# Opening of a fused adaLN/FFN kernel: longer and earlier dummy products, attention spread on GpSimd, side columns last, four low pieces of B11

## What is computed

```python
# stage 1: a mixed 1x1 convolution, per batch entry b (128 of them), x is (128, 64, 1024)
h = gelu(cond @ W0 + b0)
h = gelu(h @ W1 + b1)
att = softmax(h @ W2 + b2)                       # (128, 8)
agg_w = einsum('bk,koi->boi', att, weight)       # a 64x64 matrix for each b
agg_b = att @ bias_k
y = einsum('boi,bih->boh', agg_w, x) + agg_b[:, :, None]
# stage 2: a linear layer with 8 LoRA experts, the best 2 weighted
base = einsum('bsd,od->bso', y, base_W)          # 1024 x 1024
logits = einsum('bsd,ed->bse', y, router_W)      # 8 experts
mid = einsum('bsd,edr->bser', y, lora_A) * w_dense[..., None]
out = x + base + 2 * einsum('bser,erd->bsd', mid, lora_B)
```

## Time and profile before

| what | us |
|---|---|
| median of 3 runs | 967.26 |
| lowest and highest | 966.91, 967.41 |
| the profiled execution, whole | 968.04 |
| its span (first to last instruction) | 966.3 |
| TensorE busy in the span | 954.1 |
| VectorE busy | 739.2 |
| GpSimd busy | 294.5 |
| ScalarE busy | 236.8 |

### The profile page before, as it was taken

How to read it: one execution, slowest core, us unless ns; L and a number is a source line. 1 busy time by engine, 2 the same in 40 slices (tenths; PEclk the granted TensorE clock), 3 DMA queues, 4 the chain that set the end, 5 groups by cost and what they waited for, 6 DMA issues and landing times.

```text
span 966.3 us, 17804 instructions
## 1 busy us (share of the span) xinstructions
PE 954.1 (99%) x5765; PEld 880.7 (91%) x5765; DVE 739.2 (76%) x1641; ACT 236.8 (25%) x541; POOL 294.5 (30%) x228
## 2 busy tenths in 40 slices
PE   8999899999999999999999999999999999999997
PEld 6998799999999999999999999999999999999996
DVE  5858878777778777778777778777788777787774
ACT  5435122222122222222222222222222222222210
POOL 3002331233331333321333321333322333322331
PEclk9999999999999999999999999999999999999999
DMA  8766143332343332343333343323342323432311
GB/s 341 190 199 179 51 136 115 111 117 89 114 136 111 112 106 100 114 136 110 113 101 105 114 135 107 115 95 106 119 135 98 122 89 104 131 128 96 131 47 44
DMA packets 46693, 116.04 MB, mean 120 GB/s; under 512 B 20432, under 2 KB 20560, under 8 KB 45520
## 3 DMA queue, kind: packets, MB, share of 16 engines
q1 hardware_dynamic: 45824, 111.54, 34.6%
q0 software_dynamic: 576, 4.19, 2.2%
q10 hardware_dynamic: 272, 0.03, 0.0%
HBM read 77.97 MB, written 33.59 MB: 115 GB/s over the span
## 4 chain that ended last, share of the span: by engine, by line
PE 95%; DVE 3%; issue 1%; ACT 0%; POOL 0%; DVEq 0%; POOLq 0%; ACTq 0%
PE pc L499 17%; PE pb L510 13%; PE pa L510 12%; PE y_ps L471 11%; PE pb L513 9%; PE pa L513 9%; PE pd L499 8%; PE pc L554 4%; PE pd L554 4%; PE pc L536 1%; PE pa L524 1%; PE pd L536 1%; PE pb L524 1%; PE pd L544 1%; DVE w_lo L928 1%
## 5 line engine op out<-in xcount | busy, mean ns | idle before, releaser
L471 PE MATMUL y_ps<-mix_w,x_sb 128*128 128x128 f32 x1024 | 194.9, 276 | 0.1
L394 POOL TENSOR_TENSOR out_sb<-out_sb,u 128x512 f32<-128x512 f32 x90 | 127.8, 1449 | 202.2 <-DVE u L1109 202.2
L471 PEld LDWEIGHTS y_ps<-mix_w,x_sb 128*128 128x128 f32 x1024 | 168.6, 191 | 12.8 <-DVE ya L1014 0.5
L364 POOL TENSOR_TENSOR ya<-ya 128x512 f32<-128x512 f32 x30 | 40.4, 1345 | 384.6 <-DVE ya L1014 384.6
L1014 DVE TENSOR_TENSOR ya<-y_ps,bias_sb 128x512 f32<-128x512 f32 x128 | 87.7, 685 | 39.2 <-PE y_ps L471 35.7
L499 PE MATMUL pc<-w_hi,s_hi 128*128 128x512 f32 x240 | 99.1, 413 | 0.0
L510 PE MATMUL pa<-w_hi,a_hi 128*128 128x376 f32 x240 | 94.6, 394 | 0.7 <-ACT p L825 0.7
L499 PE MATMUL pc<-w_hi,s_lo 128*128 128x512 f32 x240 | 94.4, 393 | 0.0
L499 PE MATMUL pc<-w_lo,s_hi 128*128 128x512 f32 x240 | 93.8, 391 | 0.0
L810 ACT ACTIVATE exps<-logits,neg_max 128x8 f32<-128x8 f32 x64 | 19.3, 301 | 271.3 <-DVE neg_max L1031 271.3
L817 ACT ACTIVATE mid_hi<-pd 128x128 fp32r<-128x128 f32 x62 | 17.2, 278 | 276.1 <-PE pd L544 276.1
(11 more groups left out here) (214 smaller groups left out, 2554.7 us busy)
## 6 DMA issues: line engine op xcount, KB each, us to landing
x_sb<-in_x SPq DMA_DIRECT2D x64, 512.0 KB, 3.9
out_sb<-in_x SPq DMA_DIRECT2D x64, 512.0 KB, 4.3
out<-out_sb SPq DMA_DIRECT2D x64, 512.0 KB, 2.7
w_raw<-in_base_t SPq DMA_DIRECT2D x5, 1024.0 KB, 12.3
w_raw<-neg POOLq DMA_DIRECT2D x4, 1024.0 KB, 11.4
bias_sb<-bias_rows SPq DMA_DIRECT2D x62, 64.0 KB, 4.9
w_raw<-in_side SPq DMA_DIRECT2D x1, 544.0 KB, 8.7
lb_raw<-in_lora_b SPq DMA_DIRECT2D x1, 512.0 KB, 15.0
```

The costliest lines, as they stand in the source:

```text
L364: nc.gpsimd.tensor_tensor(y_block(0, 1), y_block(0, 1), y_block(0, 0), ALU.subtract).then_inc(s3_set, 1)
L394: nc.gpsimd.tensor_tensor(o, o, u2[:, :], ALU.add).then_inc(done, 1)
L471: mm = nc.tensor.matmul(y_ps[q % 2][:, j * P:(j + 1) * P], x_sb[m][:, c * P:(c + 1) * P], mix_w[m][:, :], start=True, stop=True)
```

## The change

Five things, all in the opening:

1. **Dummy products.** TensorE's queue begins with three products of a constant zero tile (128 columns, float32), ahead of the wait for `hot`. `keep_warm` takes the column counts: behind the second layer (512, 256) in place of one of 512, behind the third four of 512 in place of three, a new one of 512 behind the transposed attention, (512, 256) in place of one behind the bias product, and the last two, which stood between the bias rows (L456) and the mixing, are gone.
2. **`att_spread` on GpSimd**, ahead of the split of B11, and no longer on VectorE (where it stood ahead of the first `add_bias`).
3. **Low part of B11 in four pieces** of 512 columns in place of two of 1024, each with its own count of `w_lo_set[B11]`.
4. **The first product of pair 0** does its twelve heads first, then waits for `side_lo_set`, and does its twelve tails.
5. **Bias rows.** Their DMA to DRAM goes from ScalarE's queue to SP's, behind the 12 loads; ScalarE sets both mixing blocks ahead of the copy of the bias.

```diff
@@ sync
+            sp.wait_ge(bias_ready, 1)
+            sp.dma_start(bias_dram.rearrange("s (b c) -> b s c", b=B),
+                         bias_rows[:, :].rearrange("b (s c) -> b s c", s=2)).then_inc(bias_out, 16)
             sp.wait_ge(bias_out, 16)
@@ gpsimd
+            pool.wait_ge(pick_set, 5)
+            pool.wait_ge(att_step, 4)
+            nc.gpsimd.tensor_tensor(att_spread[:, :].rearrange("j (t k) -> j t k", k=K),
+                                    own_tile[:, :].unsqueeze(2).broadcast_to([P, NT, K]),
+                                    att_n[:, :].unsqueeze(1).broadcast_to([P, NT, K]), ALU.mult).then_inc(spread_set, 1)
...
-            for n in range(WP):
-                pool.wait_ge(w_hi_set[B11], n + 1)
-                nc.gpsimd.tensor_tensor(w_lo[w_piece(B11, n)], w_raw[w_piece(T2, n)],
-                                        w_hi[w_piece(B11, n)].bitcast(f32), ALU.subtract).then_inc(w_lo_set[B11], 1)
...
+            for n in range(HALF):
+                if n % (HALF // WP) == 0:
+                    pool.wait_ge(w_hi_set[B11], n // (HALF // WP) + 1)
+                nc.gpsimd.tensor_tensor(w_lo[quarter(B11, n)], w_raw[quarter(T2, n)],
+                                        w_hi[quarter(B11, n)].bitcast(f32), ALU.subtract).then_inc(w_lo_set[B11], 1)
@@ tensor
+            def keep_warm(*columns):
+
+                for n in columns:
+                    nc.tensor.matmul(pb[:, 0:n], hot[:, 0:P], hot[:, 0:n], start=True, stop=True)
+
+            zeros = nc.const_aps.tensor(0.0, (P, P))
+            for _ in range(3):
+                nc.tensor.matmul(pb[:, 0:P], zeros, zeros, start=True, stop=True)
             pe.wait_ge(hot_set, 1)
...
-            keep_warm(1)
+            keep_warm(512, 256)
             pe.wait_ge(mlp_act, 2)
             nc.tensor.matmul(mlp_ps[1][:, 0:K], h2[:, :], w2_sb, start=True, stop=True).then_inc(mlp_mm, 1)
-            keep_warm(3)
+            keep_warm(512, 512, 512, 512)
...
             nc.tensor.transpose(mlp_ps[0][0:K, 0:B], att_n[:, :], ident[:, :]).then_inc(att_tr, 1)
+            keep_warm(512)
...
             nc.tensor.matmul(bias_ps, att_t[:, :], bk_sb[:, :], start=True, stop=True).then_inc(bias_mm, 1)
-            keep_warm(1)
+            keep_warm(512, 256)
             pe.wait_ge(bias_ready, 1)
...
             mm.then_inc(bias_bc_mm, 1)
-            keep_warm(2)
@@ plain_pair
                 if first(p):
+                    for j in range(HALF):
+                        pe.wait_ge(w_lo_set[B11], j + 1)
+                        for y, w, start, stop in plain_splits(*a11, j, True):
+                            plain_head(y, w, start, stop, B11, pa, j)
                     pe.wait_ge(side_lo_set, 1)
+                    for j in range(HALF):
+                        for y, w, start, stop in plain_splits(*a11, j, True):
+                            plain_tail(y, w, start, stop, B11, pa, j, 0)
@@ scalar
-            act.wait_ge(bias_ready, 1)
-            act.dma_start(bias_dram.rearrange("s (b c) -> b s c", b=B),
-                          bias_rows[:, :].rearrange("b (s c) -> b s c", s=2)).then_inc(bias_out, 16)
-            place_mix(0, 0)
+            for m in range(2):
+                place_mix(0, m)
             act.wait_ge(bias_bc_mm, 1)
...
-            place_mix(0, 1)
```

## The result

| | median, us | lowest to highest | executions |
|---|---|---|---|
| before, beside it | 967.39 | 966.67 to 968.49 | 20 |
| changed | 968.9 | 965.17 to 973.38 | 20 |

The ratio is 1.0019, with a 95% interval from 1.001 to 1.0028: the changed kernel is slower by about 0.2%, 1.5 us by the medians and 1.8 us by the ratio. The forecast was 965.6, and 963.5 to 967.0 the range. Half of the changed kernel's executions took 969.47 us or more, which no execution of before in that series did. The one that was profiled took 968.18, span 966.4; before's took 968.04.

The account below looks back on a forecast made before the run. TensorE was taken to bound the kernel, busy 954.1 of 966.3 us. Earlier mixing (-0.79) and no wait for the side columns (-0.90) gave -1.69 us, so 965.6 us, range 963.5 to 967.0.

Parts of the forecast that it names:

- Dummies ahead of the mixing: Opening on TensorE: two dummies gone, -1.00, 256 columns more earlier, +0.21; mixing starts at 12.82, 0.79 us earlier.
- Other dummies: Opening on TensorE: they fill pauses, taken as 0, up to +0.3 us if two tight places stick out.
- Side columns last: First product of pair 0: starts without waiting for side_lo, saving 0.90 us of a wait of 0.91.
- Attention on GpSimd: Ahead of B11's split: spread taken as 1.5 us, bounds 1.30 and 2.6, hidden; no gain by itself.
- The rival in which GpSimd's last piece stands in VectorE's way: Low part of A11 takes 1.3 us longer: 966.6; chance 0.06, shared with dummies that stick out.
- Bias rows on SP's queue: Pair 1's x tile 1 lands at 34.4, asked for at 35.0: hidden by 0.6 us, where it had 3.5.
- the sum: Whole execution: -0.79 and -0.90 make -1.69 us, median 967.26 to 965.6; chance 0.42.
- its upper bound, 10.5: Pair 1's x tile 1 takes 10.5 us, landing at 35.9; as a rival 966.5, chance 0.12.
- the slower rival: Pair 1's loads sink into the accumulating DMA: tile 1 lands at 39.3, 969.9 us; chance 0.08.
- the early rise: Denser dummies lift TensorE's clock before the mixing, 1.67 us more, gain cut by tile 1 to 2.3: 965.0; chance 0.14.
- The later fall of the clock: After TensorE's pause near 106 us: 1.7 us of work lost; a rival has it go away, 963.9, chance 0.18.

Follow-up runs that it names:

- e7: e1 with the two dummies of 512 columns ahead of the mixing put back; 964.84 us, ratio 0.9965.
- e5: e1 with the early dummies as before, the two ahead of the mixing still left out; 964.26 us, ratio 0.9969.
- e2: The kernel before with only the DMA of the bias rows moved to SP's queue behind the weight loads; 968.08 us, ratio 1.0005.
- e12: The kernel before with only heads first and tails last in the first product of pair 0; 966.0 us, ratio 0.9985.
- e6: e1 with heads and tails of the first product alternating again, waiting for side_lo, and the old dummies; 965.85 us, ratio 0.998.
- e1: The changed kernel with the DMA of the bias rows issued by ScalarE again; 964.06 us, ratio 0.9964.
- e11: e1 with the attention spread on VectorE again and B11's low part in two pieces; 963.13 us, ratio 0.9964.
- e13: The changed kernel as it is, first of four more executions looked at for the long times; 971.73 us.
- e16: The changed kernel as it is, fourth of four more executions looked at for the long times; 967.89 us.
- e3: The changed kernel with GpSimd's first accumulating DMA, and so both, held until x tile 1 of pair 1 has landed; 964.41 us, ratio 0.9964.
- e10: e1 with pair 1's x tiles issued before the wait for the bias rows and the first accumulating DMA behind x tile 1; 964.01 us, ratio 0.9965.
- e14: The changed kernel as it is, second of four more executions looked at for the long times; 970.39 us.
- e15: The changed kernel as it is, third of four more executions looked at for the long times; 970.51 us.
- e9: The changed kernel as it is, measured again for the spread; 967.83 us, ratio 1.0011, profiled execution 966.16 us.
- e17: The changed kernel with only GpSimd's second accumulating DMA held until x tile 1 of pair 1 is in; 968.66 us, ratio 1.0015.

## Why the prediction was wrong

**Dummies ahead of the mixing, -0.79: right.** Mixing at 12.88 in place of 12.82. In the time of an execution it can't be told from nothing (e7).

**Other dummies, 0: right** as far as the medians tell (e5). With them `pick_half` starts at 8.24 in place of 8.19, which is the 0.05 us of that tight place. Their effect on the clock stays open: with the new dummies it rose before 9 us in 8 of 15 traces, with the old ones in none of four (before, e2, e5, e12), which is too few to tell.

**Side columns last, -0.90: the place was right, the size perhaps too small.** In the profiled execution it gave what was said, since TensorE's own mixing was next. The runs give 1.3 to 1.5 us (e12) and 1.1 to 1.8 (e6 against e5 and e1), but e12's interval holds 0.90, and those of e5 and e6 overlap. What the term lacked is seen in e6's profile: it was read from an execution in which the clock rose at about 17 us. Where it rises early VectorE is the later of the two by more, the wait is 2.05 us, and 1.5 us of slow work follow.

**Attention on GpSimd, 1.5 us, hidden: right that it is hidden**, and 1.07 us is below the lower bound of 1.30. The rival in which GpSimd's last piece stands in VectorE's way didn't come in the first profile (VectorE's low part of A11 takes 0.69 us at 18.03). It did where the clock rose early: in e6 GpSimd's last piece ends at 16.3, and VectorE's row is

```profile
15.00 1.81 DVE L1049 TENSOR_TENSOR a_lo<-ya,a_hi 128x512 fp32r<-128x512 f32 x1 [0.69 <-ACT a_hi L836]
```

In e1 it takes 1.03 us. In e11, where GpSimd is done at 15.8, it takes 0.69.

**Bias rows on SP's queue, "hidden by 0.6 us": this step failed.** It had four numbers. The write was to land at 24.4; it did at 25.0 (e13: 24.7, e16: 24.4). The Trainium skill, "DMA: Bandwidth & Descriptors", section "Queues, rings and completion order", says that each DMA engine takes the descriptors of a ring in order, and the trace agrees: the 32 KB took 14.2 us behind the loads. Tile 1 was to be issued at 25.4 to 25.7; it was at 25.92. It was to need 8.7 us; it needed 10.9. And it was asked for at 35.2 in place of 35.0. Against the sum's 25.7 the issue is 0.2 us late, and the transfer 2.2 us long: tile 1 landed at 36.8 in place of 34.4, and a cover of 0.6 us became a wait of 1.63. The 8.7 us came from a transfer of before whose issue had stood in a full queue for 1.80 us; its upper bound, 10.5, was of the same transfer with that stand. The bound was taken for a worst case, but the tile here was issued 0.75 us after the accumulating DMA, and by e3 that DMA is worth 3.3 us of it. The sentence against the slower rival, "with the queue still full of weights, 10.5 us were enough", took a transfer whose issue began 1.8 us ahead of the accumulation's for one that is issued behind it.

**The sum was too small for the rest of the change.** Without the moved DMA the gain is 3.3 us by the medians and 3.5 by the ratio (e1), not 1.69; e11 and e10 say the same. Two of the rivals are in e1's profile together, the early rise and no fall behind the pause near 106 us: 3.77 us of lead at the pause, 5.2 at the end. How often each comes in executions without a trace isn't shown.

**The slower rival was the right mechanism**, at 0.08. It placed the break-even at 36.70, and mixing in the short executions starts at 36.27 to 36.85. It foresaw a landing at 39.3 and 969.9 us; the three long executions have 37.6 to 39.0 us and 970.4 to 971.7. The rest is what no case had, the low clock behind the wait.

**The early rise, 965.0, was a rival, priced with the tile at 34.4.** It does happen, in e14 and e15, and ends at 970.4 and 970.5: an earlier TensorE waits longer, and the longer wait takes the clock. So in these executions the gain of the opening isn't only lost but turned into a loss. (The rival also left out pair 0's own tile 1, for which TensorE then waits 1.0 to 1.5 us.) Where pair 1's tile isn't late, as in e1, the rise is a gain.

**The later fall of the clock** is in the first profile (0.50 from 110 to 112 us) and not in e9's. It comes and goes in the same kernel. Those two executions differ by 2.0 us (968.18, 966.16), of which 0.6 is from the tile (36.85 less 36.27); 1.4 are left for the fall, where the forecast priced it at 1.7. Before seems to have it nearly always: of the 75 executions of before beside the experiments, four have a mean granted clock of 1.0 and took 965.3 to 965.6 us, the others 966.5 or more. What decides whether the clock falls there stays open.

**The range** came from landings between 4.3 and 10.5 us, and the text knew the cover to be 0.6 us. With a cover that small, both sides should have had like chances.

## What to carry to other kernels

When an opening gets faster, list the transfers that the next stage asks for, with issue, landing and the time they are asked for. A cover of less than a microsecond on a transfer that runs beside another large DMA is no cover. Before moving a small DMA onto a queue, see who waits on that queue for it: here a 32 KB write held back two 512 KB tiles. A wait of TensorE costs its length, and the long ones of the opening here (2.05 us in e6, 2.90 and more for the tile) also left slow work behind them. And what a change is worth in a profile with one behaviour of the clock isn't what it is worth with the other: read both before adding up.

## What the runs showed of the hardware

- TensorE came to the pace of 2.4 GHz early in some executions of the same kernel, between about 5 us (e15) and 8.5 (e14), and at about 17 in others (`pick_half` product 0.61 or 0.99 us, eight mixing matmuls 1.13 to 1.16 us or sixteen 3.73). Where it came late, the granted clock is 1.00 all the same: the first profile of the changed kernel has 1.00 from 2 us on, with matmuls twice as long until 16.4. In the opening one reads the lengths, not that column.
- An early rise need not last. In e11's profile the granted clock is 0.50 from 12 to 14 us, in e13's from 10 to 16, in e17's from 12 to 18, and all three first had the short `pick_half` product.
- After waits of 2.90, 5.25 and 5.64 us for a tile the granted clock was 0.50 and matmuls were long for some 3 to 6 us, and after one of 2.05 us for the side columns (e6) for some 3 us; after 0.8, 1.3 and 1.63 us it stayed at 1.00. After the pause of 2.2 to 2.4 us near 106 us it fell in some executions and not in others.
- A 512 KB load issued some 0.7 us behind an accumulating DMA of 1 MB took 10.7 to 13.2 us (a second one starts 5 to 7 us later beside all but e17's 10.8), 7.6 with both held back, and x tile 0, issued 0.86 us ahead of tile 1, 3.7 us. The 64 KB of bias behind it took 16.2.
- The attention spread, 128x512 from two broadcast operands, took 1.07 us on GpSimd, less than its plain sum of that size, and on VectorE, beside GpSimd's low pieces, 1.95 and 2.19 (e11).
